# Attention normalisation: four broadcast matmuls per head into one wide PSUM tile, two tiles in turn, one multiply per head

## The chip, the cores and the metric

The kernel runs as one program on all 8 cores of one Trainium2 chip, without communication between the cores. Four sequences are split in two halves each, and every core computes the output of 2048 tokens of one sequence. The metric is the device time in microseconds (us) of the slowest core.

## The reference, cut to what matters

One transformer layer with modulation from a conditioning vector: modulated layer norm, attention with 16 heads of 64 channels over 4096 tokens, projection, residual; then modulated layer norm and a gated feed-forward layer whose activations and weights go through a blockwise 4-bit quantisation.

```python
attn = jnp.einsum('bhnd,bhmd->bhnm', q, k)
attn = jax.nn.softmax(attn, axis=-1)
out = jnp.einsum('bhnm,bhmd->bhnd', attn, v)
out = out.transpose(0, 2, 1, 3).reshape(b, n, c)
return jnp.einsum('bnc,cd->bnd', out, w_proj) + b_proj
```

The change touches one step of this: the division by the softmax sum, done on `out` per head and token before the projection.

## The kernel before, in words

A core holds its tokens transposed: channels on the 128 partitions, tokens along the free axis (D = 1024 channels as KC = 8 chunks of 128, T = 2048 own tokens, N = 4096 tokens of keys). The code is emitted in phases with a barrier between them: modulation; layer norm with Q and K (L386 and L388 broadcast two rows of statistics over 128 partitions with one-row matmuls, L461 makes Q and K); V (L619); attention (L725 on, 16 heads in 8 pairs); the normalisation of the attention output (L853 to L879); the projection (L881 on); second layer norm; feed-forward.

All order is written out by hand. `em` puts an instruction on an engine, `wt` makes an engine's queue wait until a semaphore has reached a value, `dr` drains an engine, `dma` issues a transfer on a named queue, with four semaphores in turn for each queue. `mP`, `mV` and `mA` are counters that TensorE, VectorE and ScalarE raise when an instruction that carries them is done. Every queue runs in order.

During attention, the unnormalised output goes to `O` (128 partitions, 8 chunks, 2048 tokens, bf16; the even head of a pair on partitions 0 to 63, the odd one on 64 to 127), and the logarithm of each head's sum goes to a row of `lnsums`. At the end of attention SP issues the reload of `x_own` (8 MB, L852).

The normalisation is then this. ScalarE turns the 16 rows of logarithms into reciprocals, in rows 32 to 47 of `lnsums` (L856). For each of the 16 heads:

- POOL issues a small DMA (L864, issued by the helper at L128) that copies the head's row of 2048 reciprocals, 8 KB, to row 0, where TensorE can read it. It may start when the matmuls of the previous head have read row 0 (`stg_free`).
- For each of NQS = 4 pieces of QS = 512 tokens, TensorE multiplies a column of ones with the row (L868, one contraction row, 64 output partitions, float32), which spreads the reciprocals over 64 partitions of the PSUM tile `bc35`, and VectorE multiplies `O` by it in place (L873). There is one `bc35` tile of 512 columns: TensorE waits for the last multiply ahead of each matmul (`mV.v`, L867), and VectorE waits for the matmul.

The barrier at L879 ends the phase; after it POOL loads the projection's weights (L885), and TensorE's projection matmuls (L900) wait for these.

Of the kernel before, what the change touches and what calls it, by code (L numbers as in the profile page):

```python
# [7 lines left out]
F32 = mybir.dt.float32  # L8
BF16 = mybir.dt.bfloat16
I16 = mybir.dt.int16  # L10
ALU = mybir.AluOpType
# [3 lines left out]
P = 128  # L15
# [3 lines left out]
def build(cfg):  # L19
    N, D, NH, FI, SL = cfg["N"], cfg["D"], cfg["NH"], cfg["FI"], cfg["SL"]  # L20
    T = N // 2
# [5 lines left out]
    QS = 512  # L27
    NQS = T // QS
# [40 lines left out]
    def sb(name, shape, dt, stack=None):  # L69
        return (stack or es).enter_context(nc.sbuf_tensor(name, shape, dt))  # L70

    def psum(name, parts, free, dt=F32, stack=None):
        esz = 4 if dt == F32 else 2
        banks = -(-free * esz // 2048)
        return (stack or es).enter_context(
            nc.psum_tensor(name, [parts, banks * 2048 // esz], dt))
# [9 lines left out]
    mP, mV, mA = Sem("mP"), Sem("mV"), Sem("mA")  # L86
# [4 lines left out]
    ones1x = sb("ones1x", [1, P], F32)  # L91
# [16 lines left out]
    with nc.Block("mk") as blk:  # L108
# [3 lines left out]
        def em(eng, fn, inc=None, k=1):  # L112
            if inc is None:
                E[eng](fn)
                return None
            inc.v += k
            E[eng](lambda e, fn=fn, h=inc.h, k=k: fn(e).then_inc(h, k))
            return inc.v
# [8 lines left out]
        def dma(q, dst, src):  # L127
            return _q_issue(q, lambda e, dst=dst, src=src: e.dma_start(dst, src))  # L128
# [4 lines left out]
        def wtt(eng, tok):  # L133
            if tok:
                wt(eng, tok[0], tok[1])

        def qwait(eng, q):
            for s in QSEMS[q]:
                wt(eng, s, s.v)

        def wt(eng, sem, v=None):
            v = sem.v if v is None else v
            E[eng](lambda e, h=sem.h, v=v: e.wait_ge(h, v))

        def dr(eng):
            E[eng](lambda e: e.drain())  # L146

        def barrier():
            for eng in ("sync", "gpsimd", "scalar", "vector", "tensor"):
                for s in ALL_SEMS:  # L150
                    wt(eng, s)
# [84 lines left out]
        with contextlib.ExitStack() as p0:  # L236
# [24 lines left out]
            for kc in range(KC):  # L261
# [7 lines left out]
                for nt in range(2 * D // 512):  # L269
# [4 lines left out]
                        start=(kc == 0), stop=(kc == KC - 1)), mP)  # L274
# [19 lines left out]
        with contextlib.ExitStack() as p1:  # L294
# [17 lines left out]
            bc_ps = psum("bc_ps", P, SL, F32, p1)  # L312
# [234 lines left out]
        O = sb("O", [P, KC, T], BF16, p34)  # L547
        with contextlib.ExitStack() as pv:
# [58 lines left out]
            for kt in range(KT):  # L607
# [9 lines left out]
                for half in range(2):  # L617
                    for kc in range(KC):
# [4 lines left out]
                            start=(kc == 0), stop=(kc == KC - 1)),  # L623
# [101 lines left out]
        with contextlib.ExitStack() as p3:  # L725
# [6 lines left out]
            with contextlib.ExitStack() as p3i:  # L732
# [11 lines left out]
                for pp in range(NPP):  # L744
# [15 lines left out]
                    for qh in range(2):  # L760
                        exp_at = {}
                        pv_at = {}
                        for g in range(NG):
# [6 lines left out]
                            elif prev_exp:  # L770
# [4 lines left out]
                                start=True, stop=True, tile_position=(0, 0)))  # L775
# [3 lines left out]
                                start=True, stop=True, tile_position=(64, 0)), mP)  # L779
                            sc_at = mP.v  # L780
                            if g >= 2:
                                gp = g - 2
                                ktp, qs2p = divmod(gp, 2)
                                if gp == 0 and not (pp == 0 and qh == 0):
# [6 lines left out]
                                    start=(ktp == 0), stop=(ktp == KT - 1)))  # L791
# [5 lines left out]
                                                   start=(ktp == 0), stop=(ktp == KT - 1)),  # L797
# [9 lines left out]
                        for gp in (NG - 2, NG - 1):  # L807
# [6 lines left out]
                                start=False, stop=True))  # L814
# [4 lines left out]
                                start=False, stop=True), mP)  # L819
# [31 lines left out]
                    wtt("sync", pw_st[tb])  # L851
                t_xr = dma("sync", x_own[:], xr[:, :, 0:T])  # L852
            with contextlib.ExitStack() as p35:  # L853
                bc_ps = psum("bc35", P, 512, F32, p35)
                qwait("scalar", "gpsimd")
                a_rcp = em("scalar", lambda e: e.activation(  # L856
                    lnsums[32:48, :], lnsums[0:16, :], AF.Exp, scale=-1.0), mA)
                stg_free = 0
                for h in range(NH):
                    b_ = 64 * (h % 2)  # L860
                    wt("gpsimd", mA, a_rcp)
                    if stg_free:
                        wt("gpsimd", mP, stg_free)
                    t_stg = dma("gpsimd", lnsums[0:1, :], lnsums[32 + h:33 + h, :])  # L864
                    wtt("tensor", t_stg)
                    for qs in range(NQS):
                        wt("tensor", mV, mV.v)  # L867
                        p_bc = em("tensor", lambda e, qs=qs, b_=b_: e.matmul(  # L868
                            bc_ps[b_:b_ + 64, 0:512], ones1x[:, 0:64],
                            lnsums[0:1, QS * qs:QS * (qs + 1)],  # L870
                            start=True, stop=True, tile_position=(0, b_)), mP)
                        wt("vector", mP, p_bc)
                        em("vector", lambda e, qs=qs, b_=b_, h=h: e.tensor_tensor(  # L873
                            O[b_:b_ + 64, h // 2, QS * qs:QS * (qs + 1)],
                            O[b_:b_ + 64, h // 2, QS * qs:QS * (qs + 1)],
                            bc_ps[b_:b_ + 64, 0:512], ALU.mult), mV)
                        dr("vector")
                    stg_free = mP.v
            barrier()  # L879

        with contextlib.ExitStack() as p4:  # L881
# [11 lines left out]
            for oc in range(KC):  # L893
                for qs in range(NQS):
# [4 lines left out]
                    for kc in range(KC):  # L899
# [3 lines left out]
                            start=(kc == 0), stop=(kc == KC - 1)),  # L903
# [15 lines left out]
        with contextlib.ExitStack() as p5:  # L919
# [17 lines left out]
            for vec, dst in ((cb1, cbfull), (sbm, sbfull)):  # L937
# [13 lines left out]
                for half in range(D // 512):  # L951
# [3 lines left out]
                        start=True, stop=True), mP)  # L955
# [77 lines left out]
        with contextlib.ExitStack() as p6:  # L1033
# [10 lines left out]
            for th in range(2):  # L1044
                tbase = TH * th
                with contextlib.ExitStack() as pga:
# [29 lines left out]
                    for ii, (io, iw) in enumerate(isl_bounds):  # L1076
# [8 lines left out]
                        for qts in qsteps:  # L1085
# [7 lines left out]
                            for j, qt in enumerate(qts):  # L1093
                                off = 512 * j
                                for kc in range(KC):
# [4 lines left out]
                                        start=(kc == 0), stop=(kc == KC - 1)))  # L1100
                            p_gu = 0
                            for j, qt in enumerate(qts):
                                off = 512 * j
                                last_j = j == len(qts) - 1
                                for kc in range(KC):
# [4 lines left out]
                                        start=(kc == 0), stop=(kc == KC - 1)),  # L1110
# [17 lines left out]
                with contextlib.ExitStack() as pdw:  # L1128
# [4 lines left out]
                    for opp in range(2):  # L1133
                        for ic in range(FIC):
# [9 lines left out]
                            for j in range(4):  # L1144
                                for qs in range(2):
# [5 lines left out]
                                                      start=(ic == 0), stop=(ic == FIC - 1)),  # L1151
# [28 lines left out]
def _get_nc():  # L1180
    if "nc" not in _NC_CACHE:
        _NC_CACHE["nc"] = build(CFG)
    return _NC_CACHE["nc"]
# [44 lines left out]
if __name__ == "__main__":  # L1228
    nc = build(CFG)
    n = sum(1 for _ in nc.all_instructions())  # L1230
    print("built OK; instructions:", n)
```

How the kernel before makes its waits and increments, by code:

```python
        def em(eng, fn, inc=None, k=1):  # L112
            if inc is None:
                E[eng](fn)
                return None
            inc.v += k
            E[eng](lambda e, fn=fn, h=inc.h, k=k: fn(e).then_inc(h, k))
            return inc.v
# [22 lines left out]
        def wt(eng, sem, v=None):  # L141
            v = sem.v if v is None else v
            E[eng](lambda e, h=sem.h, v=v: e.wait_ge(h, v))
```

## Time and profile before

| what | us |
|---|---|
| median of 2 timed runs | 4419.11 |
| the two runs | 4397.9 and 4440.33 |
| the profiled execution's own time | 4412.29 |
| its span on the slowest core (core 1) | 4410.7 |
| spans of the 8 cores | 4378.5 to 4410.7 |

The span runs from the first to the last instruction of the slowest core; 1.6 us of the execution's time lie around it. The metric is set by the slowest core. An engine's "busy" time is the time in which its records lie; idle time ahead of an instruction is put down to what released it. One matmul of float32 operands shows as two records.

### The profile page before, as it was taken

The numbers are of one execution on the slowest core, as the hardware profiler recorded it, in microseconds if no ns is written. First come the engines' busy times: TensorE is split into PE (matmuls) and PEld (weight loads), VectorE is DVE, ScalarE is ACT, GpSimd is POOL, SyncE is SP. The second block draws the span as 40 slices with busy tenths as digits, with TensorE's granted clock in tenths as the row PEclk, the third lists the DMA queues.
The fourth block names the chain that finished last, engine by engine and source line by source line (L and its number), as shares of the span: only waits on it lengthen the run. The fifth ranks groups of instructions, "written<-read, shape, count | busy, mean of one in ns | idle before, by whom it ended". The sixth has DMA issues, their size and how long they took to land.

```text
span 4410.7 us, 32017 instructions; the slowest of 8 cores (4378.5 to 4410.7 us)
## 1 busy us (share of the span) xinstructions
PE 2230.3 (51%) x8558; PEld 707.1 (16%) x8558; DVE 2790.8 (63%) x4069; ACT 1199.3 (27%) x1239; POOL 239.7 (5%) x399
## 2 busy tenths in 40 slices
PE   3476658778787878855555600022222163222227
PEld 0122112222222222211100200011111131111113
DVE  0566561129999999999811479966666624666661
ACT  0011110088898988866500000000000000000000
POOL 1011110100111000010000000000000000000000
PEclk7687778989998999977755755566666586666658
DMA  6211115412222222222210110011111012111102
GB/s 187 69 45 42 54 64 138 109 40 56 72 72 72 51 72 70 59 77 60 66 60 7 22 30 14 14 29 29 29 29 29 22 50 68 29 29 29 29 24 86
DMA packets 270191, 235.26 MB, mean 53 GB/s; under 512 B 195136, under 2 KB 231360, under 8 KB 266944
## 3 DMA queue, kind: packets, MB, share of 16 engines
q1 hardware_dynamic: 232528, 112.83, 10.2%
q0 software_dynamic: 32816, 105.70, 8.6%
q10 hardware_dynamic: 4672, 14.68, 1.2%
q8 instruction: 75, 1.23, 0.1%
q14 instruction: 100, 0.82, 0.1%
HBM read 157.36 MB, written 46.66 MB: 46 GB/s over the span
## 4 chain that ended last, share of the span: by engine, by line
DVE 43%; PE 19%; DVEq 14%; DMA 11%; issue 5%; ACT 4%; SPq 3%; POOL 0%; ACTq 0%; POOLq 0%
DVEq L232 7%; DVEq L222 4%; PE dp_ps L1147 4%; PE bc L868 3%; PE v_ps L619 2%; SPq L131 2%; DMA wu_sb<-wuts 2%; PE g_ps L1096 2%; ACT pb L804 2%; DVEq L146 2%; DVE x_own L211 2%; DVE x_own L213 2%; DVE x_own L209 2%; DVE x_own L195 2%; DVE x_own L188 2%
## 5 line engine op out<-in xcount | busy, mean ns | idle before, releaser
L804 ACT ACTIVATE pb<-s_ps,negc 128x1024 bf16<-128x1024 f32 x1024 | 1037.2, 1230 | 115.9 <-PE s_ps L776 114.9
L1096 PE MATMUL g_ps<-wg_sb,h2q 128*128 128x512 bf16 (+1 forms) x768 | 188.8, 406 | 1283.8 <-DMA wu_sb<-wuts 1236.0
L772 PE MATMUL s_ps<-qb,kb 64*128 64x512 bf16 x1024 | 393.2, 387 | 190.2 <-ACT pb L804 121.5
L787 PE MATMUL pv_ps<-pb,vres 128*65 128x512 bf16 x992 | 413.6, 417 | 87.0 <-DVE O L838 87.0
L776 PE MATMUL s_ps<-qb,kb 64*128 64x512 bf16 x1024 | 406.3, 399 | 0.0
L1114 ACT ACTIVATE silu_sb<-g_ps 128x1024 bf16<-128x1024 f32 (+1 forms) x56 | 47.1, 841 | 1282.6 <-PE u_ps L1106 1282.6
L793 PE MATMUL pv_ps<-pb,vres 128*65 128x512 bf16 x992 | 388.6, 392 | 0.0
L1119 DVE TENSOR_TENSOR hmul<-silu_sb,u_ps 128x1024 bf16<-128x1024 bf16 (+1 forms) x56 | 55.6, 993 | 431.8 <-ACT silu_sb L1114 359.1
L1096 PEld LDWEIGHTS g_ps<-wg_sb,h2q 128*128 128x128 bf16 x768 | 82.0, 108 | 1384.8 <-issue 1318.7
L461 PE MATMUL qk_ps<-h,wqk 128*128 128x512 bf16 x768 | 213.6, 429 | 40.0 <-ACT qkst L473 25.0
L1147 PE MATMUL dp_ps<-hq,wd 128*128 128x512 bf16 x704 | 163.2, 397 | 74.1 <-DMA wd<-wdts 60.3
L772 PEld LDWEIGHTS s_ps<-qb,kb 64*128 64x128 bf16 x1024 | 94.0, 93 | 661.6 <-issue 661.6
L868 PE MATMUL bc<-lnsums,ones1x 1*64 1x512 f32 x128 | 123.8, 1068 | 132.8 <-DMA lnsums<-lnsums 87.4
L154 ACT ACT_TABLE_LOAD x5 | 6.4, 1283 | 638.3 <-issue 314.4
L1106 PE MATMUL u_ps<-wu_sb,h2q 128*128 128x512 bf16 (+1 forms) x768 | 166.3, 370 | 0.0
L787 PEld LDWEIGHTS pv_ps<-pb,vres 128*65 128x65 bf16 x992 | 108.3, 109 | 324.4 <-issue 324.4
L873 DVE TENSOR_TENSOR O<-O,bc 64x512 bf16<-64x512 bf16 x64 | 43.9, 685 | 182.5 <-PE bc L868 182.5
L473 ACT CAST qkst<-qk_ps 128x512 bf16<-128x512 f32 x96 | 56.3, 586 | 350.9 <-DVE qkn L437 304.0
L628 DVE CAST vres<-v_ps 128x1024 bf16<-128x1024 f32 x32 | 39.2, 1226 | 165.8 <-PE v_ps L619 165.8
L1159 DVE SCALAR_TENSOR_TENSOR x_own<-dp_ps,gbcol,x_own 128x512 f32<-128x512 f32 x32 | 24.0, 751 | 177.0 <-PE dp_ps L1147 174.4
L619 PE MATMUL v_ps<-wv,hld 128*128 128x512 bf16 x512 | 119.0, 386 | 23.0 <-DMA wml<-wmod 23.0
L437 DVE TENSOR_REDUCE qkn<-nrm_ps 1x1 f32<-1x512 f32 x192 | 122.1, 671 | 12.7 <-PE nrm_ps L427 11.3
(182 smaller groups left out, 3813.2 us busy)
## 6 DMA issues: line engine op xcount, KB each, us to landing
x_own<-wgate POOLq DMA_DIRECT2D x22, 512.0 KB, 4.8
x_own<-wup POOLq DMA_DIRECT2D x22, 512.0 KB, 4.8
x_own<-wdown POOLq DMA_DIRECT2D x16, 704.0 KB, 6.0
wd<-wdts SPq DMA_DIRECT2D x88, 128.0 KB, 2.1
wg_sb<-wgts SPq DMA_DIRECT2D x10, 1024.0 KB, 6.9
wu_sb<-wuts SPq DMA_DIRECT2D x10, 1024.0 KB, 9.2
xo<-x SPq DMA_DIRECT2D x4, 2048.0 KB, 15.9
hscr<-h POOLq DMA_DIRECT2D x8, 1024.0 KB, 5.3
```

Source lines behind the costliest of these rows:

```text
L222: V(lambda e: e.drain())
L232: V(lambda e: e.drain())
L461: em("tensor", lambda e, oc=oc, kc=kc, pb=pb, bi=bi: e.matmul(qk_ps[pb][:, 0:SL], wqk_sb[kc][:, P * oc:P * (oc + 1)], h_buf[bi][:, kc, :], ...
L619: em("tensor", lambda e, kt=kt, kc=kc, half=half, tb=tb: e.matmul(v_ps[tb][:, 512 * half:512 * (half + 1)], hld[tb][:, kc, :], wv_sb[kc][: ...
L772: em("tensor", lambda e, kt=kt, qoff=qoff, pb=pb, sAB=sAB: e.matmul(sAB[:, 0:512], kbuf[pb][0:64, P * kt:P * (kt + 1)], qbuf[pb][0:64, qof ...
L776: em("tensor", lambda e, kt=kt, qoff=qoff, pb=pb, sAB=sAB: e.matmul(sAB[:, 512:1024], kbuf[pb][64:128, P * kt:P * (kt + 1)], qbuf[pb][64:1 ...
L787: em("tensor", lambda e, ktp=ktp, qs2p=qs2p, gp=gp, h0=h0: e.matmul(pv_ps[0][:, 512 * qs2p:512 * (qs2p + 1)], vres[:, ktp, 65 * h0:65 * (h ...
L793: lambda e, ktp=ktp, qs2p=qs2p, gp=gp, h1=h1: e.matmul(pv_ps[1][:, 512 * qs2p:512 * (qs2p + 1)], vres[:, ktp, 65 * h1:65 * (h1 + 1)], pbuf ...
L804: exp_at[g] = em("scalar", lambda e, sAB=sAB, pAB=pAB: e.activation(pAB[:, 0:1024], sAB[:, 0:1024], AF.Exp, bias=negc[:], scale=0.125), mA)
L868: p_bc = em("tensor", lambda e, qs=qs, b_=b_: e.matmul(bc_ps[b_:b_ + 64, 0:512], ones1x[:, 0:64], lnsums[0:1, QS * qs:QS * (qs + 1)], star ...
L1096: em("tensor", lambda e, kc=kc, qt=qt, iw=iw, tb=tb, tbase=tbase, off=off: e.matmul(g_ps[tb][:, off:off + iw], h2q[:, kc, tbase + P * qt:t ...
L1147: lambda e, ic=ic, ib=ib, j=j, qs=qs: e.matmul(dp_ps[2 * j + qs][:, 0:512], wd_sb[ib][:, P * j:P * (j + 1)], hq[:, ic, 512 * qs:512 * (qs ...
```

## The change

It splits the single PSUM tile of 512 columns into two tiles of 2048 columns, one for even heads and one for odd ones, which together take all of PSUM. TensorE issues the four matmuls of a head one after the other, and only the last raises the counter. VectorE then does one multiply over all 2048 tokens of the head. TensorE's wait for VectorE is now one per head, and for the multiply of two heads earlier. The staging DMA and its wait for the previous head's last matmul stay.

```diff
-                bc_ps = psum("bc35", P, 512, F32, p35)
+                bc_ps2 = [psum(f"bc35{i}", P, T, F32, p35) for i in range(2)]
...
+                tt_done = [0, 0]
                 for h in range(NH):
                     b_ = 64 * (h % 2)
+                    hb = h % 2
                     wt("gpsimd", mA, a_rcp)
                     if stg_free:
                         wt("gpsimd", mP, stg_free)
                     t_stg = dma("gpsimd", lnsums[0:1, :], lnsums[32 + h:33 + h, :])
                     wtt("tensor", t_stg)
+                    if tt_done[hb]:
+                        wt("tensor", mV, tt_done[hb])
                     for qs in range(NQS):
-                        wt("tensor", mV, mV.v)
-                        p_bc = em("tensor", lambda e, qs=qs, b_=b_: e.matmul(
-                            bc_ps[b_:b_ + 64, 0:512], ones1x[:, 0:64],
+                        em("tensor", lambda e, qs=qs, b_=b_, hb=hb: e.matmul(
+                            bc_ps2[hb][b_:b_ + 64, QS * qs:QS * (qs + 1)],
+                            ones1x[:, 0:64],
                             lnsums[0:1, QS * qs:QS * (qs + 1)],
-                            start=True, stop=True, tile_position=(0, b_)), mP)
-                        wt("vector", mP, p_bc)
-                        em("vector", lambda e, qs=qs, b_=b_, h=h: e.tensor_tensor(
-                            O[b_:b_ + 64, h // 2, QS * qs:QS * (qs + 1)],
-                            O[b_:b_ + 64, h // 2, QS * qs:QS * (qs + 1)],
-                            bc_ps[b_:b_ + 64, 0:512], ALU.mult), mV)
-                        dr("vector")
+                            start=True, stop=True, tile_position=(0, b_)),
+                            mP if qs == NQS - 1 else None)
                     stg_free = mP.v
+                    wt("vector", mP, stg_free)
+                    tt_done[hb] = em("vector", lambda e, b_=b_, h=h, hb=hb: e.tensor_tensor(
+                        O[b_:b_ + 64, h // 2, 0:T],
+                        O[b_:b_ + 64, h // 2, 0:T],
+                        bc_ps2[hb][b_:b_ + 64, 0:T], ALU.mult), mV)
+                    dr("vector")
```

TensorE's queue before, at the first head; `bc35` is the PSUM tile, `d_gpsimd3` the semaphore of the staging DMA, `mV` VectorE's counter, and the branch rows carry the waits:

```order
L143 UNCONDITIONAL_BRANCH [waits d_gpsimd3]
L117 UNCONDITIONAL_BRANCH [waits mV]
L868 MATMUL bc35<-lnsums,ones1x 64x512
L143 UNCONDITIONAL_BRANCH
L117 UNCONDITIONAL_BRANCH [waits mV]
L868 MATMUL bc35<-lnsums,ones1x 64x512
L143 UNCONDITIONAL_BRANCH
L117 UNCONDITIONAL_BRANCH [waits mV]
L868 MATMUL bc35<-lnsums,ones1x 64x512
```

The same queue after the change, at the third head, where the even tile `bc350` comes up again:

```order
L143 UNCONDITIONAL_BRANCH [waits d_gpsimd1]
L114 UNCONDITIONAL_BRANCH [waits mV]
L871 MATMUL bc350<-lnsums,ones1x 64x512
L114 UNCONDITIONAL_BRANCH
L871 MATMUL bc350<-lnsums,ones1x 64x512
L114 UNCONDITIONAL_BRANCH
L871 MATMUL bc350<-lnsums,ones1x 64x512
L117 UNCONDITIONAL_BRANCH
L871 MATMUL bc350<-lnsums,ones1x 64x512
```

The wait for VectorE ahead of each of the four matmuls has become one ahead of the four. The DMA wait stands where it stood.

VectorE's queue after the change, first two heads; each multiply waits for TensorE's counter:

```order
L117 UNCONDITIONAL_BRANCH [waits mP]
L879 TENSOR_TENSOR O<-O,bc350 64x2048
L146 UNCONDITIONAL_BRANCH
L143 UNCONDITIONAL_BRANCH
L117 UNCONDITIONAL_BRANCH [waits mP]
L879 TENSOR_TENSOR O<-O,bc351 64x2048
```

Where four multiplies of 512 columns with four waits stood for a head, one of 2048 columns stands. The queues of POOL, SP and ScalarE hold the same instructions in the same order as before.

## Rows read from the trace of the kernel before

**Rows 1.** The page: busy us (share of the span) and instructions by engine.

```profile
PE 2230.3 (51%) x8558; PEld 707.1 (16%) x8558; DVE 2790.8 (63%) x4069; ACT 1199.3 (27%) x1239; POOL 239.7 (5%) x399
```

**Rows 2.** The chain of waits that ended last, from 2206 to 2418 us, by line.

```profile
by line: PE bc L868 58.8%; DVE O L873 16.1%; DMA lnsums<-lnsums 13.3%; issue 11.0%; DVEq L143 0.5%; POOLq L143 0.4%
```

**Rows 3.** Busy time by engine over the stage (columns as in the header).

```profile
core 1: us, PE busy (x) PEld busy (x) DVE busy (x) ACT busy (x) POOL busy (x), PEclk, DMA share, GB/s
2206.00:2418.00 212.00, 123.77 (x128) 18.14 (x128) 43.86 (x64) 0.00 (x0) 7.28 (x15) 0.50 0.09 31
```

**Rows 4.** Timeline, first to third head (start us, length us, what, idle and releaser).

```profile
2197.09 0.39 SPq L128 DMA_DIRECT2D x_own<-x  x1
...
2206.24 1.93 PE L868 MATMUL bc<-lnsums,ones1x 1*64 1x512 f32 x2 [46.19 <-DMA lnsums<-lnsums]
...
2217.37 0.50 POOL L128 DMA_DIRECT2D lnsums<-lnsums  x1 [17.39 <-PE bc L868]
2222.84 1.93 PE L868 MATMUL bc<-lnsums,ones1x 1*64 1x512 f32 x2 [6.08 <-DMA lnsums<-lnsums]
2225.72 1.94 PE L868 MATMUL bc<-lnsums,ones1x 1*64 1x512 f32 x2 [0.94 <-DVE O L873]
...
2233.52 0.69 DVE L873 TENSOR_TENSOR O<-O,bc 64x512 bf16<-64x512 bf16 x1 [2.19 <-PE bc L868]
2234.02 0.48 POOL L128 DMA_DIRECT2D lnsums<-lnsums  x1 [16.16 <-PE bc L868]
2235.93 1.08 PE L868 MATMUL bc<-lnsums,ones1x 1*64 1x512 f32 x1 [2.52 <-DMA lnsums<-lnsums]
```

**Rows 5.** The matmul line L868: its records (ns min/median/max), and its waits (us, times).

```profile
L868 PE MATMUL bc<-lnsums,ones1x x128: 1052/1067/1082, 2206.2 to 2415.6; 1*64 1x512 f32 x128
  DMA lnsums<-lnsums: 87.4, 16
  DVE O L873: 45.4, 48
```

**Rows 6.** DMA, us to landing: `lnsums` copies in attention (1000 to 2195 us); `x_own`.

```profile
DMA to landing us min/median/max: 1.5/1.6/7.9
x_own<-x SPq DMA_DIRECT2D x1, 8192.0 KB, 29.2
```

**Rows 7.** Timeline of the last multiply and of what follows the barrier.

```profile
2416.73 0.69 DVE L873 TENSOR_TENSOR O<-O,bc 64x512 bf16<-64x512 bf16 x1 [2.18 <-PE bc L868]
2418.84 2.18 POOL L128 DMA_DIRECT2D wpj_all<-wproj  x4 [14.17 <-issue]
```

**Rows 8.** Timeline, one-row matmuls of the first layer norm with the matmuls behind them.

```profile
603.83 2.04 PE L386 MATMUL bc_ps<-rs_row,ones1x 1*128 1x512 f32 x2 [5.44 <-DVE nmr_row L377]
605.66 1.91 PE L388 MATMUL bc_ps<-nmr_row,ones1x 1*128 1x512 f32 x2
607.51 3.59 PE L461 MATMUL qk_ps<-h,wqk 128*128 128x512 bf16 x8
```

**Rows 9.** Weight loads of the same place.

```profile
605.67 0.33 PEld L388 LDWEIGHTS bc_ps<-nmr_row,ones1x 1*128 1x128 f32 x1 [0.52 <-issue]
```

**Rows 10.** VectorE groups by line and shape (count; busy us, mean ns; idle).

```profile
L873 DVE TENSOR_TENSOR O<-O,bc 64x512 bf16<-64x512 bf16 x64 | 43.9, 685 | 182.5 <-PE bc L868 182.5
L195 DVE TENSOR_TENSOR x_own<-x_own 128x1408 f32<-128x1408 f32 x16 | 26.0, 1625 | 1.5 <-issue 0.4
```

**Rows 11.** Float32 matmuls L588; in the stretch: PE and PEld busy, clock, DMA.

```profile
L588 PE MATMUL mrow_ps<-wml,silu_c x128: 589/592/1061, 688.0 to 867.4; 128*1 128x512 f32 x128
...
709.00:714.00 5.00, 1.88 (x4) 0.25 (x4) 1.00 0.65 189
```

**Rows 12.** Busy time by stretch around the place of rows 8, columns as in rows 3.

```profile
603.80:607.50 3.70, 3.67 (x4) 1.16 (x4) 0.00 (x0) 0.00 (x0) 0.00 (x0) 0.50 0.02 4
607.50:611.00 3.50, 3.50 (x9) 1.03 (x8) 3.32 (x6) 0.00 (x0) 0.00 (x0) 0.50 0.00 0
611.00:613.00 2.00, 2.00 (x9) 0.73 (x9) 1.93 (x4) 0.00 (x0) 0.00 (x0) 0.71 0.00 0
```

## The prediction

> **What bounds the kernel now.** I read the page first: VectorE is busy for 63% of the span, TensorE for 51%, POOL for 5% [rows 1]. No engine is full over the whole, so what the change is worth has to be read from its own stage. The chain of waits over that stage is made of the matmul (58.8%), the multiply (16.1%), the staging DMA (13.3%) and issue time (11.0%) [rows 2]: a serial loop. The busy times say the same: in 212 us TensorE works 123.8, VectorE 43.9 [rows 3]. The reader is to see one pattern in the timeline [rows 4]: a pair of records of 1.93 us, 0.94 us in which TensorE is idle until the multiply is done (0.69 us, and two handovers of some 0.12), the next pair.
>
> That wait comes 48 times, 45.4 us in total; the wait for the staging DMA comes 16 times, 87.4 us in total [rows 5]. The first of these is not part of the stage, it holds the 46.2 us in which TensorE was idle from the end of attention on [rows 4], which leaves 41.2 us for 15 gaps. One is 6.08 us; its DMA was issued at 2217.37, while `x_own`, issued at 2197.09 [rows 4] with 29.2 us to landing [rows 6], was still coming in until about 2226. The other 14 take 35.1, so 2.51 each, as at the third head [rows 4].
>
> The stage runs from the first of these matmuls at 2206.2 us to the end of the last multiply, 2416.73 + 0.69 = 2417.4 us [rows 4, 7], so 211.2 us or 4.8% of the span. Check: 16 heads x 4 pairs x 1.93 = 123.5; + 45.4 + 41.2 = 210.1; + 0.1 handover + 0.69 last multiply = 210.9, against 211.2 measured.
>
> **The matmuls.** The change keeps all 64 matmuls, and takes away the 48 waits between the four of a head. What counts is how closely the pairs then follow. In a pair of 1.93 us with records of 1.067, the second record starts 1.93 - 1.07 = 0.86 after the first. If the eight records of a head follow at 0.86, its run takes 7 x 0.86 + 1.07 = 7.09 us. The nearest row for pairs that follow each other is the first layer norm, where one-row float32 matmuls of 512 columns stand back to back: the pair at 603.83 is followed by the pair at 605.66, that by the next matmul at 607.51 [rows 8]. That is 1.83 and 1.85 for a pair, with switches of weights and shape in them; it bounds the run from above: 3 x 1.85 + 1.93 = 7.48 us. From below, the second of those pairs shows a spacing of 1.91 - 1.06 = 0.85, and a run of 7 x 0.85 + 1.07 = 7.02 us. I take 7.09, since this is the same line with the same weights all the way.
>
> Before, a head costs 4 x 1.93 + 45.4/16 = 10.56 us. It now costs 7.09. The saving is 3.47 x 16 = 55.5 us, between 49.3 (7.48) and 56.6 (7.02).
>
> A rule speaks against part of this. Rows first: the second weight load of L388 lies at 605.67, in the first 0.33 us of a record of the same row group that began at 605.66 [rows 8, 9], and the spacing stays at 0.85: the load is hidden. The Trainium skill (TensorE: Matmul & The Clock Gate, Part 3: Packing small matmuls) says that weight loads overlap with running matmuls only when they go to another row group (its Part 2 also allows a background buffer). By that rule each of the 48 new joins would show a load, at least 18.14/128 = 0.14 us [rows 3], and 6.8 of the 55.5 us would be lost; this case's row disagrees, and the measurement decides.
>
> **The multiply.** 64 multiplies of 512 columns become 16 of 2048. TENSOR_TENSOR takes 685 ns at 512 columns and 1625 at 1408 [rows 10], so 1.05 ns per column, and 685 + 1536 x 1.05 = 2.30 us at 2048. From both sides: 2.15 us (four times 512 columns at 1.05 with no fixed part) and 2.74 (four times 685). It runs beside the staging DMA and the next head's matmuls, whose period is 7.09 + 2.51 = 9.6 us, and TensorE waits only for the multiply of two heads earlier, done some 9 us before. So 15 of 16 are hidden. The cover would be gone only if a multiply took more than one period. The last has no cover: the tail grows from 0.69 to 2.30, +1.6 us (bounds +1.5 and +2.1). The drain behind it lies in the same place as before.
>
> **The staging DMA.** Nothing of it changes: one row 0, freed by the previous head's last matmul, POOL issues, TensorE waits. It is late next: after the change TensorE idles 15 times for it, 14 x 2.51 + 6.08 = 41.2 us, nothing saved. The second DMA is now issued 3.5 us earlier, still under the load of `x_own` (the load ends at about 2226). If the third falls under it too, that costs another 6.08 - 2.51 = 3.6 us; by my times it is issued at about 2227, so I count 0 and keep 3.6 for the range.
>
> POOL's issue and the multiply now start together, at the end of the run. They met before too: POOL at 2234.02, the multiply from 2233.52 to 2234.21 [rows 4], the gap 2.52. I take no extra wait; the other end is a rival below.
>
> **Behind the stage.** POOL issues the projection's weights 1.4 us after the last multiply [rows 7], behind the same barrier. This and all later phases move up unchanged. `x_own` has landed at about 2226, and the new end of the stage is at about 2363, so nothing is uncovered.
>
> **Sum.** -55.5 + 1.6 + 0 = -53.9 us; the stage goes from 211.2 to 157.3. Against the profiled execution (4412.29, that is 4410.7 of span and 1.6 around it): 4358.4 us, a change of -1.2%. Its own time is 6.8 us below the median of the two timed runs and lies between them (4397.9 and 4440.3). I stay with 4358. About 2%, some 88 us, is what a measurement of this kernel can tell from no change, and the sum lies below it.
>
> **The rivals.**
> *The clock rises.* TensorE has a granted clock of 0.50, the 1.2 GHz level, in the whole stage [rows 3]. With runs of 7 us instead of 1.9 it might be granted 2.4 GHz. Four float32 records in a row take 1.88 us at a granted 1.00, the last 0.59 [rows 11], so 0.43 from one to the next; a head's run would take 7 x 0.43 + 0.59 = 3.60 us, 3.49 less, and the time would be 4358 - 16 x 3.49 = 4302 us. Against it: in the layer norm, 3.7 us of one-row matmuls without a gap and 3.5 us of full ones right behind them stay at 0.50; the clock rises after 611, with the full ones [rows 12]. Before those one-row matmuls the engine stood idle for 5.4 us [rows 8]. One row of 128 seems to count for little. Chance 0.05. The Trainium skill (TensorE: Matmul & The Clock Gate, Part 1: The HAM clock gate) says that sustained activity releases the half rate, and doesn't say that the number of rows matters; by that rule the runs would speed up.
>
> *The staging DMA is held up by the multiply.* If POOL can't prepare its DMA while the long multiply runs, each of 15 gaps grows by the difference 2.30 - 0.69 = 1.6 us: 24 us, time 4382. For it: both start on the same event. Against it: the `lnsums` copies that were issued during attention, beside VectorE instructions of up to 1.6 us [rows 10], landed after a median of 1.6 us [rows 6], and the third head's trip here takes 1.91 from issue to matmul [rows 4]. Chance 0.10.
>
> *The change doesn't take the wait away.* If the 0.94 us were TensorE's own issue time, it would stay between the matmuls and the time with it: 4412 + 1.6 = 4414. For it: 11.0% of the chain is "issue". Against it: 0.94 is 0.1 + 0.69 + 0.1, and the pairs of rows 8 follow without a gap. Chance 0.06.
>
> *Slower.* The staging trip as the only place where loss can arise: a copy from one partition to the same memory that competes with VectorE's in-place writes of 2048 columns. The longest landing of such a copy is 7.9 us against 1.6 [rows 6]. If all 15 took that, 15 x 6.3 = 94.5 us would be added: 4358 + 94 = 4452 us. It decides from 53.9/15 = 3.6 us a trip. Against it: the one long gap here, 6.08 us, comes with a large load under way, and none runs after 2226. Chance 0.03.
>
> **How the numbers follow.** Forecast 0.76, held-up DMA 0.10, no effect 0.06, clock 0.05, slower 0.03. The terms' bounds give 4357 to 4369 for the forecast alone; the two timed runs lie 21 us to either side of their middle, which is wider than every term. So the range is 4326 to 4398: it takes in the held-up DMA, and leaves out the clock, the slower case and no effect, and a little of the spread. Faster by over 2%: the clock's 0.05 and 0.08 for two medians that fall apart by another 0.8%: 0.13. Slower by over 2%: 0.02. The rest, 0.85, is within 2%.
>
> **What would show it.** In the changed profile the stage should take 157 us. The matmul line should show 128 records of 1.06 us in 16 runs of 7.1 us; its wait for the multiply should be gone, the wait for the staging DMA should still total some 87 us (46 of it ahead of the first head). 16 multiplies of 2.3 us should sum to 37 us instead of 43.9. The granted clock should stay at 0.50. Runs of 3.6 us at 1.00 would prove the clock rival right, gaps of 4.1 us the held-up DMA, joins of 1.0 us or more the weight loads. If the stage is 54 us shorter and the time is not, a later phase has taken it back, which nothing in this trace suggests.

## The result and the profile after

The changed kernel takes 4349.35 us (median of 11 runs, 4341.5 to 4383.5) against 4405.5 us for the one before (median of 10). The ratio is 0.9866, with a 95% interval of 0.9832 to 0.9901: a gain of 1.3%, 44 to 74 us. A twelfth execution on record, at 4384.8, isn't among the eleven; with it the median is 4350.4. The forecast was 4358 us and -53.9 us. In some executions of any of these kernels the cores of one die, or of both, show a lower granted clock and take up to about 2% longer, which is why three of e5's six executions are left out of its median below, and why no time is given for e3, e4, e6 and e8b, whose only execution was of this kind.

The stage can be read far more closely than the whole. On core 1, the core of the rows of before, the matmul line L868 has become L871 and the multiply L873 has become L879. First the two lines with their records (ns min/median/max) and waits (us, times), core 1, changed kernel:

```profile
L871 PE MATMUL bc<-lnsums,ones1x x128: 1052/1056/1082, 2200.3 to 2353.1; 1*64 1x512 f32 x128
...
  issue: 172.5, 112
  DMA lnsums<-lnsums: 57.2, 4
  DVE O L879: 29.7, 12
...
L879 DVE TENSOR_TENSOR O<-O,bc x16: 2278/2286/2292, 2207.5 to 2354.2; 64x2048 bf16<-64x2048 bf16 x16
```

The records are as many as before and as long to 11 ns (median 1056 against 1067 ns) [rows 5], the 48 waits for the multiply are gone, and 57.2 + 29.7 = 86.9 us of waits are left. Of these, 45.9 lie ahead of the first head, so 41.0 us lie in the 15 gaps, against 41.2 before. Twelve gaps carry the multiply's name; whether it is to blame is a question for the experiments. The timeline of the second and third heads of the same core (start us, length us, what, idle before and releaser):

```profile
2213.19 7.06 PE L871 MATMUL bc<-lnsums,ones1x 1*64 1x512 f32 x8 [5.84 <-DMA lnsums<-lnsums]
...
2220.35 2.29 DVE L879 TENSOR_TENSOR O<-O,bc 64x2048 bf16<-64x2048 bf16 x1 [10.62 <-PE bc L871]
2220.85 0.48 POOL L128 DMA_DIRECT2D lnsums<-lnsums  x1 [12.40 <-PE bc L871]
...
2222.72 7.05 PE L871 MATMUL bc<-lnsums,ones1x 1*64 1x512 f32 x8 [2.48 <-DVE O L879]
```

Eight records now stand as one run of 7.06 us, where [rows 4] had four pairs with 0.94 us between them. The busy times of the stage, same core (columns as in rows 3):

```profile
2200.00:2357.00 157.00, 112.85 (x128) 26.12 (x128) 36.56 (x16) 0.00 (x0) 7.27 (x15) 0.50 0.11 42
```

And the chain of waits over the same stretch:

```profile
by line: PE bc L871 72.0%; DVE O L879 19.0%; DMA lnsums<-lnsums 9.2%; issue 3.0%; POOLq L143 0.2%; DVEq L143 0.2%
```

The stage takes 156.2 us on core 1 (from 2200.29 to 2354.25 + 2.29) instead of 211.2: 55.0 us less. The page of the changed kernel, which shows core 4, has the shares of the engines of before to within one point of the span [rows 1]; VectorE's is 64%.

```profile
PE 2224.0 (51%) x8558; PEld 715.7 (16%) x8558; DVE 2784.2 (64%) x4021; ACT 1199.5 (28%) x1239; POOL 239.2 (6%) x399
```

The profiled execution itself is 67.8 us shorter (4344.5 against 4412.3), with another core as the slowest. On core 1 the span is 73.4 us shorter: 55.0 are the stage, 5.9 lie ahead of it and 12.5 behind it, in parts that the change doesn't touch. These parts vary by as much from core to core: the first broadcast matmul comes between 2190 and 2206 us on the eight cores of before, and between 2182 and 2203 after; from the end of the stage to the end of the span it is 1976 to 1993 us before, and 1979 to 1983 after. So the gain that is accounted for is the 55 us of the stage, and the medians (56.2 us apart) agree with it.

### The profile page after: what moved, and what is told of

Same layout as the page of the kernel before. It is cut to its first block, busy times and chain, and to the rows that moved or that the text cites. A ratio compares the mean times of both kernels' runs of the same rounds, so it can differ in the third digit from the quotient of the medians.

```text
span 4343.0 us, 31823 instructions; the slowest of 8 cores (4318.5 to 4343.0 us)
## 1 busy us (share of the span) xinstructions
PE 2224.0 (51%) x8558; PEld 715.7 (16%) x8558; DVE 2784.2 (64%) x4021; ACT 1199.5 (28%) x1239; POOL 239.2 (6%) x399
## 4 chain that ended last, share of the span: by engine, by line
DVE 42%; PE 20%; DVEq 14%; DMA 10%; issue 5%; ACT 5%; SPq 3%; POOL 0%; ACTq 0%; POOLq 0%
DVEq L232 8%; DVEq L222 4%; PE dp_ps L1152 4%; ACT pb L804 3%; PE bc L871 3%; PE v_ps L619 3%; SPq L131 2%; PE g_ps L1101 2%; DVEq L146 2%; DMA wu_sb<-wuts 2%; PE u_ps L1111 2%; DVE x_own L211 2%; DVE x_own L213 2%; DVE x_own L209 2%; DVE x_own L195 2%
## 5 line engine op out<-in xcount | busy, mean ns | idle before, releaser
L871 PE MATMUL bc<-lnsums,ones1x 1*64 1x512 f32 x128 | 112.9, 1059 | 86.8 <-DMA lnsums<-lnsums 56.7
L879 DVE TENSOR_TENSOR O<-O,bc 64x2048 bf16<-64x2048 bf16 x16 | 36.6, 2286 | 134.1 <-PE bc L871 134.1
```

Source lines behind the costliest of these rows:

```text
L871: em("tensor", lambda e, qs=qs, b_=b_, hb=hb: e.matmul(bc_ps2[hb][b_:b_ + 64, QS * qs:QS * (qs + 1)], ones1x[:, 0:64], lnsums[0:1, QS * qs ...
```

## The experiments

What was open: whether the 48 waits alone make the gain; whether the wide multiply and the second tile have a part in it; what holds the remaining gap of 2.5 us; and whether the clock would rise. The measure in all runs is the stage, from the first broadcast matmul to the end of the last multiply, taken from the trace of each core. The stage has a granted clock of 0.50 in every run, so it can be compared throughout.

| run | stage us, eight cores | typical gap between heads us | time us |
|---|---|---|---|
| before | 211.2 to 213.3 | 2.48 to 2.51 | 4405.5 |
| changed | 156.2 to 157.9 | 2.48 to 2.51 | 4349.4 |
| e1 four multiplies | 154.8 to 156.1 | 2.47 to 2.51 | 4340.7 (one run) |
| e2 one tile | 157.3 to 158.8 | 2.54 | 4352.1 (one run) |
| e3 two tiles, double multiply | 158.0 to 160.2 | 2.47 to 2.51 | |
| e4 one tile, double multiply | 189.7 to 190.8 | 4.75 | |
| e5 three staging rows | 80.5 to 81.9 | none | 4271.5 (3 runs) |
| e6 staging by ScalarE's queue | 151.6 to 153.4 | 2.10 to 2.16 | |
| e7 selector | 57.3 | none | 4247.2 (6 runs) |
| e8b e5 in another order | 108.5 | none | |
| e9 two banks | 154.8 to 156.1 | 2.48 to 2.52 | 4339.4 (one run) |
| e10 selector, two row groups | 30.1 | none | 4224.3 (6 runs) |

**Is the wide multiply part of the gain? (e1)** It takes the four multiplies back and leaves the rest.

```diff
-                            mP if qs == NQS - 1 else None)
-                    stg_free = mP.v
-                    wt("vector", mP, stg_free)
-                    tt_done[hb] = em("vector", ... O[..., 0:T] * bc_ps2[hb][..., 0:T] ...)
+                            mP)
+                        wt("vector", mP, p_bc)
+                        tt_done[hb] = em("vector", ... one piece of 512 columns ...)
+                    stg_free = mP.v
```

> Two tiles of 2048 columns as in the changed kernel, but four multiplies of 512 columns per head again, each waiting for its own matmul. Stage = first broadcast matmul to end of last multiply; 156.2 us on core 1 and 157.2 on core 4 in the changed kernel. Theory A (the 48 waits of TensorE were the cost, the width of the multiply is worth nothing): run of a head 7.06 us, gap to the next 2.5 us, stage 155 us (last tail 0.8 instead of 2.4). Rival B (the wide multiply brings part of the gain: fewer VectorE instructions and handovers): stage at least 10 us longer, up to the old 211. Rival C (the gap of 2.5 us is now set by the end of the 2.29 us multiply, as the releaser in the trace says): gap falls below 2.5, by up to 1.6 us, stage 130 to 150.

Timeline of one head, core 7 of e1:

```profile
2231.53 7.05 PE L871 MATMUL bc<-lnsums,ones1x 1*64 1x512 f32 x8 [2.47 <-DMA lnsums<-lnsums]
2233.57 0.69 DVE L877 TENSOR_TENSOR O<-O,bc 64x512 bf16<-64x512 bf16 x1 [3.72 <-PE bc L871]
2235.63 0.69 DVE L877 TENSOR_TENSOR O<-O,bc 64x512 bf16<-64x512 bf16 x1 [1.37 <-PE bc L871]
...
2241.06 1.93 PE L871 MATMUL bc<-lnsums,ones1x 1*64 1x512 f32 x2 [2.48 <-DMA lnsums<-lnsums]
```

The run is 7.05 us and the gap 2.48 us as with the wide multiply, and the stage is shorter by 1.4 us on core 1 and by 1.6 us in the mean of the eight cores (0.9 to 2.6), since the last multiply is shorter (0.69 us instead of 2.29). So the width is worth nothing and costs the tail, and rival B falls. Rival C falls too: the last multiply of a head now ends 0.8 us after the run, and the gap hasn't moved. The name DVE on twelve gaps of the changed kernel is a coincidence of times: the multiply of the head before ends at 2220.35 + 2.29 = 2222.64, just ahead of the matmul at 2222.72, though TensorE waits for one that was done a head earlier. The view puts a wait down to what came last.

**Is the second tile part of it, and from where would it be? (e2, e3, e4)** e2 has one tile of 2048 columns, with TensorE waiting for the multiply of the head before. e3 and e4 put a second multiply of equal size, into a scratch buffer, ahead of each; e3 has the two tiles, e4 the one. The first cut is in e2 and e4, the second in e3 and e4.

```diff
-                bc_ps2 = [psum(f"bc35{i}", P, T, F32, p35) for i in range(2)]
+                bc_ps2 = [psum("bc35", P, T, F32, p35)] * 2
...
-                    if tt_done[hb]:
-                        wt("tensor", mV, tt_done[hb])
+                    if tt_done[1 - hb]:
+                        wt("tensor", mV, tt_done[1 - hb])
```

```diff
                     wt("vector", mP, stg_free)
+                    em("vector", ... qbuf[0][b_:b_ + 64, 0:T] = O[...] * bc_ps2[hb][...] ...)
                     tt_done[hb] = em("vector", ...)
```

> One tile of 2048 columns for all heads, one wide multiply; TensorE waits for the multiply of the head just before. Theory A (the staging DMA takes 2.5 us after a run, the multiply 0.1 + 2.29 + 0.1 = 2.5, so the multiply is hidden even so): gaps 2.5 to 2.6 us, stage 156 to 159. Rival D (the second tile is part of the gain): the wait for the multiply comes on top, gaps 4 us and more, stage 180 or more.

> The changed kernel with a second multiply of the same size (into a scratch buffer) ahead of each multiply: VectorE 4.6 us per head. Theory A: hidden under a period of 9.5 us, gaps stay 2.5 us; only the tail grows, stage 158 to 159. Rival C (the multiply's end sets the gap): gaps grow to 4.8 us, stage 190.

> One tile and the doubled multiply. Theory A: now the multiplies stick out: gap 0.1 + 4.6 + 0.2 = 4.9 us instead of 2.5, 14 times (the second head's gap of 5.8 us covers it), stage 156 + 34 + 2 = about 192. Rival C expects the same 190 here as with two tiles.

Timelines of core 7, first e3, then e4:

```profile
2222.63 2.28 DVE L879 TENSOR_TENSOR qb<-O,bc 64x2048 bf16<-64x2048 bf16 x1 [5.04 <-PE bc L871]
2223.12 0.49 POOL L128 DMA_DIRECT2D lnsums<-lnsums  x1 [9.05 <-PE bc L871]
2224.83 2.27 DVE L883 TENSOR_TENSOR O<-O,bc 64x2048 bf16<-64x2048 bf16 x1
2224.99 7.05 PE L871 MATMUL bc<-lnsums,ones1x 1*64 1x512 f32 x8 [2.47 <-DMA lnsums<-lnsums]
```

```profile
2235.36 2.28 DVE L879 TENSOR_TENSOR qb<-O,bc 64x2048 bf16<-64x2048 bf16 x1 [7.31 <-PE bc L871]
2235.85 0.48 POOL L128 DMA_DIRECT2D lnsums<-lnsums  x1 [11.32 <-PE bc L871]
2237.56 2.27 DVE L883 TENSOR_TENSOR O<-O,bc 64x2048 bf16<-64x2048 bf16 x1
2239.98 7.05 PE L871 MATMUL bc<-lnsums,ones1x 1*64 1x512 f32 x8 [4.73 <-DVE O L883]
```

In e3 the next run starts at 2224.99, 2.1 us before the second multiply ends (2224.83 + 2.27): with two tiles even 4.6 us of VectorE per head are hidden, and the gap stays at 2.47. In e4 the run waits for the end of the second multiply, and the gap is 4.73 us. With a multiply of single length the one tile costs 2.54 - 2.48 = 0.06 us a gap on core 7 (e2), and 0.03 where the gap had been 2.51. So the second tile brings 1 us here in the mean of the cores; it begins to matter where multiply and handovers are longer than the gap that the staging trip leaves, and with the doubled multiply it is worth 30 to 32 us on each core (e4 less e3).

e9 goes on from there: two tiles of one bank each, used in turn by the pieces, four multiplies per head (shown against e1).

```diff
-                bc_ps2 = [psum(f"bc35{i}", P, T, F32, p35) for i in range(2)]
+                bc_ps2 = [psum(f"bc35{i}", P, QS, F32, p35) for i in range(2)]
...
                     for qs in range(NQS):
+                        qb_ = qs % 2
+                        if tt_done[qb_]:
+                            wt("tensor", mV, tt_done[qb_])
```

> One staging row, heads in the old order, two tiles of 512 columns (two banks of PSUM instead of all eight), used in turn by the pieces; TensorE waits for the multiply of two pieces earlier, four multiplies per head. Theory A (0.69 us of multiply and 0.2 of handovers fit under the 1.71 us of the matmul between): run 7.1 us, gap 2.5, stage 155 us as e1_four_mults. Rival L (the many waits cost TensorE time of its own, 0.1 us or more each): stage 160 or more.

```profile
2233.26 7.05 PE L872 MATMUL bc<-lnsums,ones1x 1*64 1x512 f32 x8 [2.46 <-DMA lnsums<-lnsums]
2235.30 0.69 DVE L878 TENSOR_TENSOR O<-O,bc 64x512 bf16<-64x512 bf16 x1 [3.71 <-PE bc L872]
```

The run is again 7.05 us and the stage 154.8 us. The whole gain of the change can be had with two banks of PSUM instead of eight; the waits ahead of each matmul, already fulfilled when it comes to them, cost TensorE nothing that shows. This is also the barest proof of the cause: against the kernel before, e9 differs only in a second bank and in TensorE's wait, which is for the multiply of two pieces earlier instead of the last one.

**What is in the gap? (e6)** The staging DMA from ScalarE's queue instead of POOL's.

```diff
-                    t_stg = dma("gpsimd", lnsums[0:1, :], lnsums[32 + h:33 + h, :])
+                    t_stg = dma("scalar", lnsums[0:1, :], lnsums[32 + h:33 + h, :])
```

> The changed kernel with the staging DMA issued by ScalarE's queue, idle at this time, instead of POOL's. It measures how much of the 2.5 us gap belongs to POOL. Theory A1 (POOL's handling of about 0.5 us ahead of the transfer is on the path and ScalarE's is shorter): gap 2.0 to 2.4 us, stage 149 to 155. Rival G (the trip is the transfer itself): gap 2.4 to 2.6, stage 156. Rival H (POOL's DMA is slowed by the multiply that starts with it): gap under 2.0 us.

```profile
2256.97 2.28 DVE L879 TENSOR_TENSOR O<-O,bc 64x2048 bf16<-64x2048 bf16 x1 [6.87 <-PE bc L871]
2257.00 0.51 ACTq L128 DMA_DIRECT2D lnsums<-lnsums  x1
2258.95 3.64 PE L871 MATMUL bc<-lnsums,ones1x 1*64 1x512 f32 x4 [2.09 <-DMA lnsums<-lnsums]
```

ScalarE issues 0.03 us after the multiply starts, POOL 0.50 us after it [rows 4]; from issue to matmul it takes 1.95 us here and 1.91 in rows 4. The gap falls to 2.10, so 0.4 us of it had been POOL's late issue. The trip itself stays. That a longer multiply holds the DMA up is ruled out by the gaps of e1, the changed kernel and e3: 2.48 us beside 0.69, 2.29 and 4.6 us of multiply. Why POOL issues half a microsecond after the end of the run was not tested; in every run with POOL's queue a multiply starts at that moment.

**What if the gap goes? (e5, e8b)** Three staging rows in turn, two of them in buffers that attention has left.

```diff
+                rows = [lnsums[0:1, :], kbuf[0][0:1, :].bitcast(F32), kbuf[1][0:1, :].bitcast(F32)]
...
-                    if stg_free:
-                        wt("gpsimd", mP, stg_free)
-                    t_stg = dma("gpsimd", lnsums[0:1, :], lnsums[32 + h:33 + h, :])
+                    if row_free[h % 3]:
+                        wt("gpsimd", mP, row_free[h % 3])
+                    row = rows[h % 3]
+                    t_stg = dma("gpsimd", row, lnsums[32 + h:33 + h, :])
```

> The changed kernel with three staging rows in turn (two of them in buffers that attention has left), so that the DMAs of the next heads run under the matmuls. Theory A (what is left between the runs is the staging trip): the gaps vanish except perhaps one or two near the start; 16 runs of 8 x 0.853 = 6.85 us, stage 110 to 117 us at a granted clock of 0.50, time about 40 us under the changed kernel, 4309. Rival E (long activity of one-row matmuls does raise the clock): after a few us without a gap the granted clock goes to 1.00 and the stage falls to 60 to 70 us. Rival F (the gap is TensorE's or POOL's own handling per head): gaps of 1 us or more stay, stage 130 or more.

This missed. The gaps vanished, but the stage is 81 us, where Theory A had 110 to 117 and the clock rival at most 70. The time missed as well: 4271.5 us against an expected 4309; the ratio to the kernel before is 0.9719 (0.9654 to 0.9785). Core 7, busy times and timeline:

```profile
2195.00:2276.00 81.00, 78.08 (x128) 23.09 (x128) 36.56 (x16) 0.00 (x0) 6.29 (x13) 0.50 0.22 80
```

```profile
2227.23 1.06 PE L874 MATMUL bc<-lnsums,ones1x 1*64 1x512 f32 x1
2227.30 1.08 PE L874 MATMUL bc<-kb,ones1x 1*64 1x512 f32 x1
2228.08 1.06 PE L874 MATMUL bc<-lnsums,ones1x 1*64 1x512 f32 x1
2228.18 1.06 PE L874 MATMUL bc<-kb,ones1x 1*64 1x512 f32 x1
2228.93 1.06 PE L874 MATMUL bc<-lnsums,ones1x 1*64 1x512 f32 x1
```

The granted clock is 0.50 and a record lasts 1.06 us as ever, but two rows of records run side by side, 0.07 to 0.10 us apart, one from each staging row: an even head, which writes output partitions 0 to 63, and an odd one, which writes 64 to 127. The even head's records began at 2223.79, so the one at 2228.93 is its seventh, the first of its fourth matmul: the odd head's first matmul (2227.30) starts ahead of it, though it stands behind it in TensorE's queue. That gave a new theory, and e8b tests it by the order of the heads alone, with a wait for the last attention casts ahead of the first head; rows and tiles still go in turn:

```diff
-                for h in range(NH):
+                for i_h, h in enumerate(list(range(0, NH, 2)) + list(range(1, NH, 2))):
```

> e5_three_rows again, but the heads in the order 0, 2, ... 14, 1, 3, ... 15, so that heads that follow each other write the same 64 output partitions; the tiles go in turn as before. Theory J (in e5 the matmuls of an even and an odd head ran at the same time in the two column halves of the array, which brought its stage from the expected 112 to 81 us): no overlap here but at the one place where 14 is followed by 1; records 0.853 us apart, stage 16 x 6.83 + 2.4, less up to 5 for that place: 106 to 113 us, granted clock 0.50. Rival K (the matmuls themselves got faster without gaps, whatever half they use): stage about 81 again.

```profile
2203.00:2312.00 109.00, 106.10 (x128) 27.86 (x128) 36.56 (x16) 0.00 (x0) 6.29 (x13) 0.50 0.17 60
```

108.5 us, the same on all eight cores: with heads of one half behind each other, 128 records need 106.1 us (with some overlap at the one place where head 14 meets head 1); with the halves in turn, 78.1. The column halves are the cause. Why e5 doesn't get down to half of 106 was not tested, but its trace names the next wait:

```profile
2230.95 2.28 DVE L882 TENSOR_TENSOR O<-O,bc 64x2048 bf16<-64x2048 bf16 x1 [3.80 <-PE bc L874]
2233.34 0.28 PEld L874 LDWEIGHTS bc<-kb,ones1x 1*64 1x64 f32 x2 [0.67 <-issue]
2234.46 2.29 DVE L882 TENSOR_TENSOR O<-O,bc 64x2048 bf16<-64x2048 bf16 x1 [1.23 <-PE bc L874]
2236.87 0.28 PEld L874 LDWEIGHTS bc<-lnsums,ones1x 1*64 1x64 f32 x2
```

The next even head begins at 2233.34, 0.11 us after the wide multiply of the even head before has ended (2233.23), and the next odd head at 2236.87, 0.12 us after that of the odd one (2236.75). Each half has a single wide tile, so run and multiply alternate on it: 7.06 + 0.1 + 2.29 + 0.12 = 9.6 us for two heads, eight times that is 76.6, and the odd heads run 3.5 us behind. That makes 80.1 of the 80.5 us of this core. By this reading the wide multiply is no longer hidden here, and its width costs time; no run put four multiplies per head beside e5's rows.

**A version without staging (e7, e10).** A float32 selector of ones and zeros, made once from the identity matrix, picks the two rows of a pair of heads and spreads them over 128 partitions; the 16 rows of reciprocals are used where ScalarE writes them.

```diff
+                sel = qbuf[0][:].bitcast(F32)
+                v_sel = em("vector", lambda e: e.tensor_copy(
+                    sel[32:48, :].rearrange("p (h m) -> p h m", m=64),
+                    ident32[32:48, 32:48, None].broadcast_to([16, 16, 64])), mV)
...
+                for hp in range(NH // 2):
...
+                        em("tensor", lambda e, qs=qs, hp=hp, hb=hb: e.matmul(
+                            bc_ps2[hb][:, QS * qs:QS * (qs + 1)],
+                            sel[32:48, P * hp:P * (hp + 1)],
+                            lnsums[32:48, QS * qs:QS * (qs + 1)],
+                            start=True, stop=True, tile_position=(32, 0)),
```

> No staging at all: the 16 rows of reciprocals stay where ScalarE writes them, and a 16 x 128 float32 selector of ones and zeros per pair of heads picks two rows and spreads them over all 128 partitions; 8 pairs x 4 matmuls and 8 multiplies of 128 x 2048. Theory A (a float32 matmul of 512 columns costs 1.71 us whatever its rows and output partitions; the trips and half of the matmuls go): 8 runs of 6.85 = 55 us, plus 2.4 us tail, stage 57 to 58 us at a granted clock of 0.50; the first matmul comes 5 us sooner after the reciprocals. Time about 4349 - 99 - 5 = 4245 us. Rival E (with 16 rows of the array in use and no gaps the clock rises): stage 30 to 40 us, VectorE's 8 x 2.4 = 19 us still under it. Rival I (16 rows and 128 output columns load slower or the multiply at 128 partitions takes longer): stage 70 or more.

```profile
2190.00:2248.00 58.00, 54.94 (x64) 21.04 (x64) 18.30 (x8) 0.00 (x0) 0.00 (x0) 0.50 0.42 145
```

The stage is 57.3 us on every core, and the time 4247.18 us, ratio 0.9653 (0.96 to 0.9707). Sixteen rows and 128 output columns cost the matmul nothing (54.94 us for 64 records), and 128 partitions cost the multiply nothing (18.30/8 = 2.29 us). e10 keeps a second copy of the reciprocals and of the selector at partitions 96 to 111, and lets the pieces use row groups 32 and 96 in turn (shown against e7):

```diff
+                        r_ = (32, 96)[qs % 2]
...
-                            sel[32:48, P * hp:P * (hp + 1)],
-                            lnsums[32:48, QS * qs:QS * (qs + 1)],
-                            start=True, stop=True, tile_position=(32, 0)),
+                            sel[r_:r_ + 16, P * hp:P * (hp + 1)],
+                            lnsums[r_:r_ + 16, QS * qs:QS * (qs + 1)],
+                            start=True, stop=True, tile_position=(r_, 0)),
```

> e7_selector with the reciprocals and the selector also at partitions 96 to 111, and the four matmuls of a pair alternately from rows 32 and 96 of the array. Theory J carried over (matmuls in different row groups run at the same time, as those in different column halves did): a pair of heads takes 3.4 us instead of 6.83, stage 27 + 2.4 + up to 2 = 30 to 34 us, 25 us under e7; the second ScalarE pass costs 1.9 us ahead; time 4247 - 23 = about 4224 us. Rival M (row groups don't overlap for float32): stage 57 us, time 2 us above e7.

Busy times around the stage, and its start, both core 7:

```profile
2185.00:2220.00 35.00, 27.68 (x64) 11.27 (x64) 18.30 (x8) 2.68 (x2) 0.55 (x1) 0.50 0.67 240
```

```profile
2185.80 1.91 ACT L866 ACTIVATE lnsums<-lnsums 16x2048 f32<-16x2048 f32 x1
2187.95 12.32 PE L877 MATMUL bc<-lnsums,qb 16*128 16x512 f32 x28 [41.05 <-ACT lnsums L866]
2191.84 2.29 DVE L884 TENSOR_TENSOR O<-O,bc 128x2048 bf16<-128x2048 bf16 x1 [12.29 <-PE bc L877]
2195.26 2.29 DVE L884 TENSOR_TENSOR O<-O,bc 128x2048 bf16<-128x2048 bf16 x1 [1.13 <-PE bc L877]
```

The 64 records take 27.7 us instead of 54.9, a pair of heads every 3.4 us, and the stage 30.1. The kernel takes 4224.28 us: the best version. The ratio to the kernel before is 0.954 (0.9487 to 0.9592), but that kernel took 4439.8 us in the executions taken beside e10, 34 us more than above. Against its 4405.5 the best version has 4.1%, where the change had 1.3%, and 4.1% is also what the stage gives (211 to 30 us). What TensorE waits for next stands behind the stage:

```profile
2234.96 0.59 PE L909 MATMUL pj_ps<-O,wpj_all 128*128 128x512 bf16 x1 [19.33 <-DMA wpj_all<-wproj]
```

It idles 19.3 us for the projection's weights, which are issued only after the barrier, as it did for 18.7 us in the kernel before (core 1). No run here moves that load.

## Why the prediction was right

- **What bounds the stage.** Right. The serial loop of matmul, multiply and staging DMA was the whole stage; the pairs closed up when the waits went, and e1 and e9 show that the waits alone did it.
- **The matmuls.** A run of 7.09 us was predicted, 7.06 is measured, so a head saves 3.50 us instead of 3.47. The spacing of 0.86 within a pair carried over to the joins. The bound from above by the layer norm's pairs (7.48) was not needed.
- **The weight loads.** With a load of 0.14 us at each of the 48 joins the 16 runs would have taken 16 x 7.09 + 6.8 = 120.2 us; they took 112.85. The measurement stands by the row, and against the rule that the prediction quoted from the Trainium skill (TensorE: Matmul & The Clock Gate, Part 3: Packing small matmuls).
- **The multiply.** 2.30 us from the slope of two shapes, 2.286 measured; 15 of 16 hidden, the tail paid in full (1.60 us, as predicted). The slope came from a float32 multiply of 128 partitions without a PSUM operand; that it would hold for this one was not shown beforehand, and there was some luck in it.
- **The staging DMA.** 41.2 us predicted in gaps, 41.0 measured, with one long gap (5.84 us) under the load of `x_own` as before. In both kernels the DMA engines are full just then (share 0.99 to 1.04) and empty by the third trip; that the load is the cause is read from this, not tested.
- **The sum.** The stage shrank by 55.0 us on core 1 against 53.9. The forecast of 4358.4 stands 9.1 us over the median of 4349.35; 6.8 of it is the base, since the kernel before measured 4405.5 over ten runs and the profiled execution 4412.3, and 2.3 is the change itself (56.2 against 53.9).
- **The rivals.** The clock stayed at 0.50. The DMA was not held up: the gap is 2.48 us with a multiply of 0.69 us, with one of 2.29, and with two of together 4.6 (e1, changed, e3). The wait did go. Of the slower case nothing shows: the longest gap is 5.84 us on core 1 and 7.2 on any core, the others 2.5.
- **What the prediction didn't see.** It rightly said that the staging trip is late next, but took the remaining loop as given. It also said that the second tile lets TensorE run ahead of VectorE, and never asked whether one would do: the gap is as long as the handover, the multiply and the handover back (0.1 + 2.29 + 0.1), so it does (e2). Nor did it see that heads in different column halves can overlap once the gap between them is gone (e5).

## What to carry to other kernels

When an engine waits for its consumer between equal pieces, count what the consumer needs against what the producer takes: here two buffers of one piece were enough, since the piece (1.71 us of matmul) was longer than multiply and handovers (0.9), and wider tiles only lengthened the tail. When such a wait goes, look at the next one in the same loop before calling it done; here the gaps of the staging copy were another 41 us, and moving the selection into a matmul removed copy, loop and half of the matmuls (99 us of the stage). A releaser named in a wait is the last event and need not be the cause; change that event alone and see whether the wait moves.

## What the runs showed of the hardware

- Float32 matmuls into different column halves of the array run at the same time: the same 128 records took 78.1 us with the halves in turn (e5) and 106.1 with them one behind the other (e8b). A matmul in one half then started 1.6 us before one in the other half that stood ahead of it in the queue (e5). Matmuls in different row groups do so as well: 54.9 us in one group, 27.7 in two (e7, e10). The Trainium skill (TensorE: Matmul & The Clock Gate, Part 3: Packing small matmuls) describes both kinds of overlap; on these the runs agree, and I had not applied it to heads that follow each other.
- The granted clock stayed at 0.50, the 1.2 GHz level, through 106 us of one-row matmuls without a pause (e8b) and 55 us of matmuls with 16 rows (e7). In the layer norm it rose, to a mean of 0.71 over 2 us, while full 128-row bf16 matmuls ran [rows 12]; which difference between them and these streams counts was not separated. The Trainium skill (TensorE: Matmul & The Clock Gate, Part 1: The HAM clock gate) says that activity releases the half rate, and doesn't name the rows; these two streams, unbroken as they were, didn't raise it.
- A float32 matmul of 512 columns costs the same with 1 row and 64 output partitions as with 16 rows and 128: records of 1056 ns, 0.86 us apart, in both (e1: eight in 7.05 us; e7: 64 in 54.94 us).
- A staging copy of 8 KB within SBUF takes 1.9 us from issue to the matmul that waits for it, from POOL's queue and from ScalarE's alike (1.91 in rows 4, 1.95 in e6); POOL issues it 0.5 us later (0.50 us after the multiply's start, against 0.03).
